# Attention stage of a four-stage kernel: the order in which SyncE writes and reads back two transposed tiles

## The chip, the cores and the metric

The kernel runs on one core of a Trainium2 chip. The metric is the device time of one execution in microseconds (us); lower is better. Engines are called PE (TensorE), DVE (VectorE), ACT (ScalarE), POOL (GpSimd) and SP (SyncE). SP computes nothing; it waits on semaphores and issues DMAs.

## The reference

The program is a chain of four residual blocks on x of shape (2, 2048, 256): a gated scan, a feed-forward block with ternary weights, a second-order linear attention, and the feed-forward block again. The change lies in the attention (16 heads of 64, here with T = 2048):

```python
def step(carry, qkv):
    S_K, C_QV, G = carry
    q_t, k_t, v_t = qkv
    k_C = jnp.einsum('bhk,bhkv->bhv', k_t, C_QV)
    G = G + k_t[..., :, None] * k_C[..., None, :]
    S_K = S_K + k_t[..., :, None] * k_t[..., None, :]
    C_QV = C_QV + q_t[..., :, None] * v_t[..., None, :]
    S_C = jnp.einsum('bhkj,bhjv->bhkv', S_K, C_QV)
    o_t = jnp.einsum('bhk,bhkv->bhv', q_t, S_C - G)
    return ((S_K, C_QV, G), o_t)
_, outs = jax.lax.scan(step, (S_K0, C_QV0, G0), (q, k, v))
```

## The kernel before, in words

The attention is computed in 32 chunks of 64 tokens (`CHUNKS`), both batch entries and all 8 pairs of heads at once. For chunk j, PE first computes scores A from the keys and queries (`scores_of`, L1187) in `first_group`, then the products with the two running states (`by_states`, L1198 and L1202), then `u_and_s` (L1213), which gives u and the change of the state S. DVE masks scores A (`mask_scores`, L1599), ACT copies u^T out of PSUM into `ut` (L1486). Between these parts PE computes the projections of keys, queries and values for coming chunks, and the output product of an earlier chunk (`out_product`, L1247 to L1249). After `u_and_s` come `o_by_scores` (L1224) and scores B (L1187 again). The change of the state Z (`change_z`, L1235) for chunk j is computed at the start of chunk j + 2.

Two operands are needed with tokens on partitions, while they are computed with features on partitions: the keys of each chunk, and u. Both are transposed in two steps. DVE transposes within blocks of 32x32 (`turn_keys(j + 1)`, L1609, and `turn_u(j)`, L1616, in that order, in each chunk j). SP then moves the blocks: it writes the turned tile of 512 KB to a scratch tensor in DRAM with one DMA (`save_k`, `save_u`, both L1063), waits until that has landed, and reads it back with four DMAs of 128 KB (`land_k`, `land_u`, both L1069). ACT at last copies the landed blocks into their places (L1497): `store_k_rows(j)` writes `krow`, which `u_and_s(j)` reads, and `store_u_rows(j - 1)` writes `urow`, which `change_z(j - 1)` reads in chunk j + 1.

Keys are written from and read back into the same tile (`k32`; the trace calls it `k`, the rows of instruction order `k_75`). The turned u lies in `turned`, which is the same memory as scores A (`sc_and_k` in the rows); so DVE's first masking of scores A in chunk j + 1 waits until the write of u of chunk j is over (`u_saved`).

All of this is written out by hand as one in-order program for each engine, with counting semaphores between them; nothing reorders it. On SP, in chunk j, the order is: write the keys of j + 1, write u of j, read back the keys of j + 1, read back u of j. Each step begins with its own wait: L1062 for the DVE transposes, L1067 for the write.

In an odd chunk j the keys of chunk j + 1 have only just been projected when DVE turns them, shortly ahead of u. In an even chunk j they come out of a projection of the chunk before, and DVE turns them several us ahead of u.

Of the kernel before, what the change touches and what calls it, by code (L numbers as in the profile page):

```python
# [25 lines left out]
CHUNKS = T // CHUNK  # L26
# [10 lines left out]
def hybrid_kernel(nc, x_d, gamma_d, wqkva_d, wq_d, wk_d, wv_d, wo_d, w1_d, b1_d, w2_d, b2_d, out_d):  # L37
# [12 lines left out]
    with outer:  # L50
# [68 lines left out]
        def rows(b, i, c=0, n=1):  # L119

            return xres[:, bass.ds((i * CH + (b * TILES + c)) * D, n * D)]
# [818 lines left out]
        def attention(before):  # L940
# [58 lines left out]
            LAST_STATE = CHUNKS - 1  # L999
# [59 lines left out]
            def sync(sp):  # L1059
                def save_turned(scratch, tile, ready, saved, count):  # L1060

                    sp.wait_ge(ready, 2 * (count + 1))  # L1062
                    sp.dma_start(scratch, tile.rearrange("p t m d -> p t (m d)")).then_inc(saved, 16)  # L1063

                def land_rows(scratch, tile, saved, landing, count):

                    sp.wait_ge(saved, 16 * (count + 1))  # L1067
                    for t in range(4):
                        sp.dma_start(tile[t * 32:(t + 1) * 32, :, :, :].rearrange("p r m d -> p r (m d)"),  # L1069
                                     scratch.rearrange("(r p) t c -> t p r c", r=4)[t]).then_inc(landing, 16)  # L1070

                def save_k(j):
                    save_turned(rows_dram["k"], k32, k_turned, k_saved, j)

                def land_k(j):
                    land_rows(rows_dram["k"], k32, k_saved, k_landed, j)

                def save_u(j):
                    if j:
                        sp.wait_ge(u_landed, 64 * j)  # L1080
                    save_turned(rows_dram["u"], turned, u_turned, u_saved, j)

                def land_u(j):
                    if j:
                        sp.wait_ge(urow_done, 2 * j)
                    land_rows(rows_dram["u"], landed, u_saved, u_landed, j)

                save_k(0)
                land_k(0)
                for j in range(CHUNKS):  # L1090
                    if j + 1 < CHUNKS:
                        save_k(j + 1)
                    if j < LAST_STATE:
                        save_u(j)
                    if j + 1 < CHUNKS:
                        land_k(j + 1)
                    if j < LAST_STATE:
                        land_u(j)
                    if j == CHUNKS - 4:
                        sp.wait_ge(q_ready, 4 * KQ_BLOCKS)  # L1100
                        sp.dma_start(w1t_again[:, :, :].rearrange("p a b -> p (a b)").bitcast(FP32), w1t_dram).then_inc(w1_loaded, 16)
                sp.wait_ge(v_ready, 2 * CHUNKS)
                sp.dma_start(wv_hi[:, :, :].rearrange("p a b -> p (a b)").bitcast(FP32), w2t_dram).then_inc(w2_loaded, 16)
                for i in range(NBLK):
                    for b in range(B):
                        for j in range(2):
                            sp.wait_ge(d_xadd[b], 2 * i + j + 1)
                            sp.dma_start(out_view[b, :, i * CH + 2 * j:i * CH + 2 * j + 2, :],
                                         rows(b, i, 2 * j, 2).rearrange("p (n d) -> p n d", d=D)).then_inc(stored, 16)
                sp.wait_ge(w1_loaded, 16)  # L1110
                sp.wait_ge(w2_loaded, 16)
                sp.wait_ge(wq_loaded, 32)
                sp.wait_ge(stored, 16 * 2 * B * NBLK)
                sp.wait_ge(k_landed, 64 * CHUNKS)
                sp.wait_ge(u_landed, 64 * LAST_STATE)
# [479 lines left out]
            def vector(dve):  # L1595
# [186 lines left out]
                for j in range(2):  # L1782
                    add_down(TASKS - 1, j)

            return Stage(sync, gpsimd, tensor, scalar, vector)


# [68 lines left out]
```

## Time and profile before

| | |
|---|---|
| median of 3 runs | 1033.69 us (1032.54 to 1034.43) |
| profiled execution, its own time | 1031.72 us |
| its span in the trace | 1030.0 us |
| granted TensorE clock | 1.00 throughout |
| PE busy | 1003.6 us, 97% |
| DVE, ACT busy | 616.6 us, 491.8 us |
| mean share of the 16 DMA engines | 28.0% for the data queue |

The span counts from the first to the last instruction in the trace; the execution's own time is 1.72 us longer. Attention takes about 240 to 900 us of the span, with a chunk every 20 to 21 us. "Issue" in the chain of work and in the waits is idle time of PE for which the trace knows no semaphore.

### The profile page before, as it was taken

To read this page: it belongs to the slowest core of one execution; us is meant where nothing else is said; L and a number is where in the kernel's file an instruction comes from. 1 tells how busy PE (TensorE), PEld (TensorE's weight loads), DVE (VectorE), ACT (ScalarE), POOL (GpSimd) and SP (SyncE) were. 2 spreads that over 40 slices of the span, in tenths; PEclk is the share of its full clock that TensorE was granted. 3 is DMA by queue.
4 is the path that set the end of the run, shared out by engine and by line. 5 is a ranking of instruction groups with operands and counts; after the bars stand their busy time and mean duration, and the time that the engine had idled before them with its cause. 6 is when DMAs were issued, how large, how long until landed. Compare 5 with 4: busy or idle time off the path is not lost.

```text
span 1030.0 us, 41963 instructions
## 1 busy us (share of the span) xinstructions
PE 1003.6 (97%) x19166; PEld 906.8 (88%) x19166; DVE 616.6 (60%) x1252; ACT 491.8 (48%) x925; POOL 111.5 (11%) x130
## 2 busy tenths in 40 slices
PE   8999999999999999999999999999999999999998
PEld 6888798999988998899889989998899988889897
DVE  7888877763445544555465554563564457767773
ACT  5676766643343433343444334333443344456663
POOL 2461331220000000000000000000000000113130
PEclk9999999999999999999999999999999999999999
DMA  9422000023324323342234233422343343200101
GB/s 316 154 57 82 1 2 1 1 83 111 119 85 121 110 85 105 105 122 89 85 120 131 86 105 105 126 85 85 105 138 93 106 125 110 80 22 21 42 31 52
DMA packets 60735, 92.75 MB, mean 90 GB/s; under 512 B 7056, under 2 KB 50448, under 8 KB 59536
## 3 DMA queue, kind: packets, MB, share of 16 engines
q1 hardware_dynamic: 60288, 90.07, 28.0%
q8 instruction: 151, 2.47, 1.0%
q14 instruction: 24, 0.20, 0.1%
q10 hardware_dynamic: 272, 0.00, 0.0%
HBM read 48.63 MB, written 41.42 MB: 87 GB/s over the span
## 4 chain that ended last, share of the span: by engine, by line
PE 94%; DVE 2%; ACT 2%; issue 2%; DMA 0%; POOL 0%; SPq 0%; ACTq 0%; DVEq 0%; POOLq 0%
PE bank L223 7%; PE bank L224 6%; PE bank L225 6%; PE bank L1187 6%; PE bank L1213 6%; PE bank L1198 5%; PE bank L1247 4%; PE bank L1235 3%; PE bank L1177 3%; PE bank L1224 3%; PE bank L805 3%; PE bank L807 3%; PE bank L1248 3%; PE bank L1249 3%; PE bank L1263 3%; PE bank L1179 3%
## 5 line engine op out<-in xcount | busy, mean ns | idle before, releaser
L1473 ACT COPY qt<-bank 128x512 f32<-128x512 f32 x64 | 37.6, 587 | 149.3 <-PE bank L225 149.3
L1609 DVE STREAM_TRANSPOSE k<-kt 128x512 f32<-128x512 f32 x64 | 43.4, 697 | 108.8 <-ACT kt L1468 59.0
L1468 ACT COPY kt<-bank 128x512 f32<-128x512 f32 x64 | 37.6, 587 | 116.5 <-PE bank L225 116.5
L1630 DVE TENSOR_TENSOR state_s<-bank,state_s 128x256 f32<-128x256 f32 x124 | 46.7, 419 | 73.5 <-ACT ut L1486 71.5
L1247 PE MATMUL bank<-wo_hi,ot_hi 128*128 128x256 f32 x256 | 74.9, 293 | 0.8 <-issue 0.8
L223 PE MATMUL bank<-ln_xhi,wq_hi 128*128 128x256 f32 x256 | 75.4, 295 | 0.0
L223 PE MATMUL bank<-ln_xhi,wk_hi 128*128 128x256 f32 x256 | 75.2, 294 | 0.0
L1198 PE MATMUL bank<-qt,state_s 64*64 64x64 f32 x2048 | 69.5, 220 | 3.2 <-issue 3.2
L1623 DVE TENSOR_TENSOR state_z<-bank,state_z 128x512 f32<-128x512 f32 x62 | 39.9, 685 | 54.4 <-PE bank L1235 54.3
L1520 ACT ACTIVATE D_hidden<-bank,b_sb 128x512 f32<-128x512 f32 x64 | 44.1, 690 | 59.3 <-PE bank L1264 59.3
L224 PE MATMUL bank<-ln_xlo,wq_hi 128*128 128x256 f32 x256 | 72.4, 283 | 0.1
L225 PE MATMUL bank<-ln_xhi,wq_lo 128*128 128x256 f32 x256 | 72.3, 282 | 0.0
L1202 PE MATMUL bank<-qt,state_z 64*64 64x64 f32 x2048 | 70.2, 221 | 1.7 <-issue 1.7
L224 PE MATMUL bank<-ln_xlo,wk_hi 128*128 128x256 f32 x256 | 71.8, 281 | 0.0
L225 PE MATMUL bank<-ln_xhi,wk_lo 128*128 128x256 f32 x256 | 71.7, 280 | 0.0
L1248 PE MATMUL bank<-wo_lo,ot_hi 128*128 128x256 f32 x256 | 71.6, 280 | 0.0
L1198 PEld LDWEIGHTS bank<-qt,state_s 64*64 64x64 f32 x2048 | 64.5, 135 | 7.9 <-issue 3.9
L1249 PE MATMUL bank<-wo_hi,ot_lo 128*128 128x256 f32 x256 | 71.3, 279 | 0.0
L898 DVE TENSOR_TENSOR B_hid_lo<-B_hidden,B_hid_hi 128x512 fp32r<-128x512 f32 x64 | 54.7, 877 | 21.3 <-ACT B_hid_hi L844 21.1
L1202 PEld LDWEIGHTS bank<-qt,state_z 64*64 64x64 f32 x2048 | 64.9, 135 | 2.4 <-issue 2.1
L805 PE MATMUL bank<-w2t,B_hid_hi 128*128 128x256 f32 x256 | 63.0, 282 | 0.7 <-DVE B_hid_lo L898 0.7
L857 ACT ACTIVATE B_hidden<-bank,b_sb 128x512 f32<-128x512 f32 x64 | 44.2, 692 | 39.1 <-PE bank L788 26.0
(161 smaller groups left out, 2919.3 us busy)
## 6 DMA issues: line engine op xcount, KB each, us to landing
k_rows_scratch<-k SPq DMA_DIRECT2D x32, 512.0 KB, 2.9
k<-k_rows_scratch SPq DMA_DIRECT2D x128, 128.0 KB, 3.5
u_rows_scratch<-sc_and_k SPq DMA_DIRECT2D x31, 512.0 KB, 3.1
landed<-u_rows_scratch SPq DMA_DIRECT2D x124, 128.0 KB, 3.3
out_dram<-xres SPq DMA_DIRECT2D x16, 256.0 KB, 2.1
xres<-in_L_attn_a_x_dram SPq DMA_DIRECT2D x7, 512.0 KB, 9.8
w_nat<-in_L_ffn_W_dram SPq DMA_DIRECT2D x2, 1024.0 KB, 9.6
raw<-in_L_attn_b_W_q_dram SPq DMA_DIRECT2D x1, 1024.0 KB, 12.1
```

Of the source, the lines that this page charges most:

```text
L223: nc.tensor.matmul(out, w_hi, x_hi, start=(k == 0), stop=False)
L224: nc.tensor.matmul(out, w_hi, x_lo, start=False, stop=False)
L225: return nc.tensor.matmul(out, w_lo, x_hi, start=False, stop=(k == last_k))
L805: nc.tensor.matmul(dst, hid_hi[:, b, f, c * P:(c + 1) * P], w2t[:, f, :], start=(f == 0), stop=False)
L898: nc.vector.tensor_tensor(hid_lo[:, b, f, :], hidden[:, f % 4, :], hid_hi[:, b, f, :].bitcast(FP32), ALU.subtract).then_inc(hlow_done, 1)
L1187: last = nc.tensor.matmul(bank[bank_of[h]][half(b), p * CHUNK:(p + 1) * CHUNK], keys(p, h, b), qt[half(h), j // 2 % 2, p, j % 2, b, :], st ...
L1198: last = nc.tensor.matmul(bank[UB[b][p // 4]][half(h), u_cols(p, 0)], state_s[half(h), b, p, :], qt[half(h), j // 2 % 2, p, j % 2, b, :], ...
L1202: last = nc.tensor.matmul(bank[OB[b]][half(1 - h), cols], state_z[half(h), b, p, :], qt[half(h), (j - 1) // 2 % 2, p, (j - 1) % 2, b, :], ...
L1213: last = nc.tensor.matmul(bank[UB[b][p // 4]][half(h), u_cols(p, 0, n)], krow[half(b), p, half(h)], sc_and_k[half(b), 0:n, p, h, :], start ...
L1247: nc.tensor.matmul(dst, ot_hi[:, p, :], w[0], start=(p == 0), stop=False)
L1248: nc.tensor.matmul(dst, ot_hi[:, p, :], w[1], start=False, stop=False)
L1249: last = nc.tensor.matmul(dst, ot_lo[:, p, :], w[0], start=False, stop=(p == PAIRS - 1))
```

## The change

On SP, in each chunk, the four reads of the turned keys are moved ahead of the write of u. No instruction is added or removed on any engine, and no other engine's program changes.

```diff
                 for j in range(CHUNKS):
                     if j + 1 < CHUNKS:
                         save_k(j + 1)
+                        land_k(j + 1)
                     if j < LAST_STATE:
                         save_u(j)
-                    if j + 1 < CHUNKS:
-                        land_k(j + 1)
-                    if j < LAST_STATE:
                         land_u(j)
```

The next rows are SP's instructions in chunks 0 and 1 of the loop, as a difference between the two kernels (`k_75` is the keys' tile, `landed` the one into which u is read back).

```order
 L1063 DMA k_rows_scratch<-k_75 128x1024 [waits C_kturned]
+L1069 DMA k_75<-k_rows_scratch 32x4x256 [waits C_ksaved]
+L1069 DMA k_75<-k_rows_scratch 32x4x256 x3
 L1063 DMA u_rows_scratch<-sc_and_k 128x1024 [waits C_uturned]
-L1069 DMA k_75<-k_rows_scratch 32x4x256 [waits C_ksaved]
-L1069 DMA k_75<-k_rows_scratch 32x4x256 x3
 L1069 DMA landed<-u_rows_scratch 32x4x256 [waits C_usaved]
 L1069 DMA landed<-u_rows_scratch 32x4x256 x3
```

The wait for the keys' write (`C_ksaved`) and the four reads behind it now stand ahead of the wait for the turned u (`C_uturned`) and of u's write.

The same place in every later chunk, first before and then of the changed kernel; u's write waits there for its read of the chunk before as well (`C_uland`), and its reads for the copies out of `landed` (`C_urow`).

```order
L1063 DMA k_rows_scratch<-k_75 128x1024 [waits C_kturned]
L1063 DMA u_rows_scratch<-sc_and_k 128x1024 [waits C_uturned,C_uland]
L1069 DMA k_75<-k_rows_scratch 32x4x256 [waits C_ksaved]
L1069 DMA k_75<-k_rows_scratch 32x4x256 x3
L1069 DMA landed<-u_rows_scratch 32x4x256 [waits C_usaved,C_urow]
L1069 DMA landed<-u_rows_scratch 32x4x256 x3
```

```order
L1063 DMA k_rows_scratch<-k_75 128x1024 [waits C_kturned]
L1069 DMA k_75<-k_rows_scratch 32x4x256 [waits C_ksaved]
L1069 DMA k_75<-k_rows_scratch 32x4x256 x3
L1063 DMA u_rows_scratch<-sc_and_k 128x1024 [waits C_uturned,C_uland]
L1069 DMA landed<-u_rows_scratch 32x4x256 [waits C_usaved,C_urow]
L1069 DMA landed<-u_rows_scratch 32x4x256 x3
```

Here too only the four reads of the keys have moved, past one write.

## Rows read from the trace of the kernel before

**Rows 1.** The page: busy time, and the chain that ended last by engine

```profile
PE 1003.6 (97%) x19166; PEld 906.8 (88%) x19166; DVE 616.6 (60%) x1252; ACT 491.8 (48%) x925; POOL 111.5 (11%) x130
...
PE 94%; DVE 2%; ACT 2%; issue 2%; DMA 0%; POOL 0%; SPq 0%; ACTq 0%; DVEq 0%; POOLq 0%
```

**Rows 2.** PE's waits, 220 to 880 us: total us, times, longest

```profile
PE bank L1187 <- issue: 5.0, 3, 1.9
PE bank L1198 <- issue: 3.2, 3, 1.5
PE bank L1202 <- issue: 1.7, 3, 0.9
```

**Rows 3.** Chain of work in order of time: start us, length us, what

```profile
300.10 0.92 issue
...
421.29 1.42 issue
509.37 0.82 issue
...
711.16 1.90 issue
800.21 0.45 issue
```

**Rows 4.** DMA issues of the page: KB each, median us to landing

```profile
k_rows_scratch<-k SPq DMA_DIRECT2D x32, 512.0 KB, 2.9
k<-k_rows_scratch SPq DMA_DIRECT2D x128, 128.0 KB, 3.5
u_rows_scratch<-sc_and_k SPq DMA_DIRECT2D x31, 512.0 KB, 3.1
```

**Rows 5.** Timeline of SP, 505 to 545 us (chunks 13 and 14)

```profile
514.95 0.34 SPq L1063 DMA_DIRECT2D k_rows_scratch<-k  x1
517.95 0.34 SPq L1063 DMA_DIRECT2D u_rows_scratch<-sc_and_k  x1
518.33 2.28 SPq L1069 DMA_DIRECT2D k<-k_rows_scratch  x4
521.18 2.80 SPq L1069 DMA_DIRECT2D landed<-u_rows_scratch  x4
531.51 0.34 SPq L1063 DMA_DIRECT2D k_rows_scratch<-k  x1
538.95 0.34 SPq L1063 DMA_DIRECT2D u_rows_scratch<-sc_and_k  x1
539.33 2.38 SPq L1069 DMA_DIRECT2D k<-k_rows_scratch  x4
```

**Rows 6.** Timeline of DVE, the same stretch

```profile
526.65 1.28 DVE L1599 TENSOR_TENSOR sc_and_k<-bank,causal 128x512 f32<-128x512 f32 x2
...
537.57 1.29 DVE L1616 STREAM_TRANSPOSE sc_and_k<-ut 128x512 f32<-128x512 f32 x2
```

**Rows 7.** ACT, 220 to 880 us: its wait, and two copies of the timeline

```profile
ACT sc_and_k L1497 <- DMA k<-k_rows_scratch: 10.2, 10, 3.7
...
525.01 1.14 ACT L1497 COPY sc_and_k<-k 128x512 f32<-128x512 f32 x2
...
537.03 1.16 ACT L1497 COPY urow<-landed 128x512 f32<-128x512 f32 x2
```

**Rows 8.** Timelines of SP and DVE, 838 to 905 us (chunk 30)

```profile
869.66 0.34 SPq L1063 DMA_DIRECT2D k_rows_scratch<-k  x1
872.37 0.34 SPq L1063 DMA_DIRECT2D u_rows_scratch<-sc_and_k  x1
...
878.90 1.28 DVE L1599 TENSOR_TENSOR sc_and_k<-bank,causal 128x512 f32<-128x512 f32 x2
```

**Rows 9.** Busy by stretch, 290 to 840 us, and instruction packets in it

```profile
290.00:840.00 550.00, 540.73 (x14115) 497.26 (x14119) 287.37 (x575) 216.25 (x434) 8.50 (x14) 1.00 0.35 106
...
q8 instruction: 112, 1.84, 1.4%
```

**Rows 10.** Timeline, chunk 12: u's write on SP, PE behind its gap

```profile
496.79 0.34 SPq L1063 DMA_DIRECT2D u_rows_scratch<-sc_and_k  x1
...
510.19 0.21 PE L1198 MATMUL bank<-qt,state_s 64*64 64x64 f32 x1 [0.82 <-issue]
```

## The prediction

> **What bounds the kernel now.** I read the page first. PE is busy for 97% of the span and makes up 94% of the chain that ended last; DMA and SP's queue have 0% of that chain [rows 1]. So a change in SP's order can save only what PE loses, and cost only what PE does not lose yet.
>
> Next I read PE's own waits in the attention, 220 to 880 us. Three lines with nine waits hold 5.0 + 3.2 + 1.7 = 9.9 us, all "issue" [rows 2]. No semaphore is behind them. The chain of work in order of time says where they are; five of the pieces are at 300.10, 421.29, 509.37, 711.16 and 800.21 us [rows 3].
>
> What are they? From 290 to 840 us PE ran 14115 matmuls and 14119 weight loads, and the DMA view counts 112 packets of the kind "instruction", 1.84 MB, in the same stretch [rows 9]. That is 28234 / 112 = 252 PE instructions and 16 KB per packet: PE's program is fed through the DMA engines, a packet every 4.9 us on average. The gap before L1198 at 510.19 us stands in the middle of a run of identical matmuls, so no operand can be missing there [rows 10]. I take the gaps to be PE at the end of its fed instructions: a packet came late while the data queue was full, and the short 64x64 matmuls of `by_states` and of the scores then ate the rest. This reading is an inference, and the rest of my forecast hangs on it.
>
> The third view is SP's timeline of two chunks. In odd chunk 13 the keys' write goes out at 514.95, u's write at 517.95, the keys' reads at 518.33 and take 2.28 us to issue, u's reads at 521.18 us. In even chunk 14 the keys' write goes out at 531.51, u's at 538.95, and the keys' reads only at 539.33 us, though their data had been in DRAM for some 4.5 us [rows 5].
>
> **The change part by part.** No instruction is added, so all costs are shifts in time.
>
> *Keys in even chunks.* A 512 KB keys' write lands 2.9 us after its issue and a read 3.5 us after its own [rows 4]. The reads would be issued at 531.51 + 3.0 = 534.5 instead of 539.33, 4.8 us earlier, and be landed by 534.5 + 2.3 + 3.5 = 540.3. The only reader is ACT's copy into `krow` in the next chunk; it waited for these DMAs ten times, 10.2 us in total, at most 3.7 [rows 7]. ACT's waits are not on the path: PE waits on no ACT copy of L1497 in rows 2. Worth: 0 us, at most 10.2 us off ACT's idle time.
>
> *u in even chunks.* The reads are issued over by 536.8, and u is turned at 537.57 + 1.29 = 538.86 [rows 6], so u's write still goes at 538.95. Worth 0 us.
>
> *u in odd chunks.* The wait for the keys' write ends at 514.95 + 3.0 = 517.95; four reads at 2.28 us push u's write to 520.2 or 520.3, 2.3 us later than now. Behind it on SP stand u's reads and the next chunk's keys' write; the latter waits for DVE until 531.51 and has room. Who waits for u's write: DVE's mask of scores A in chunk 14, which starts at 526.65 [rows 6]. The write takes 3.1 us [rows 4], so it is over at 523.4, 3.2 us in time. Who waits for u's reads: ACT's copy at 537.03 [rows 7]; issued from 523.4 over 2.8 us and landed by 529.7, they have 7 us left. Worth 0 us; if that cover were gone, it would cost DVE, and a masking that is late has still a projection on PE between itself and `u_and_s`.
>
> *The tightest place is chunk 30,* where projections run out: keys' write at 869.66, hence u's write at 869.66 + 3.0 + 2.3 = 875.0 instead of 872.37, over at 878.1; the mask starts at 878.90 [rows 8]. 0.8 us is left. If the write took 1 us more, the price would be 0.2 us, once.
>
> *Keys in odd chunks.* Reads go 0.4 us earlier and no longer behind u's 512 KB. ACT's copy of them at 525.01 [rows 7] needs nothing sooner. 0 us.
>
> *The feed of PE's instructions.* Here the order matters. Today u's write, the keys' reads and u's reads form one unbroken burst in every chunk. In even chunks the change takes the keys' reads out of it and puts them where the queue is empty; u's write has then nothing behind it for 3.1 us. In odd chunks the burst is 2.3 us longer, since SP issues keys' reads before u's write where it had both in flight together. The trace of before has no row for an instruction packet against a u write alone. The bounds for even chunks: nothing (the packet waits for the write as before), or the packet comes earlier by as much as the issue of the keys' reads takes, 2.3 us [rows 5], which would close all five gaps of rows 3. By SP's timeline these five follow even chunks; they sum to 0.92 + 1.42 + 0.82 + 1.90 + 0.45 = 5.5 us. I take 0.6 us for each, an estimate: the packet no longer waits for the part of the keys' reads that is in flight with u's write, a quarter of the 2.3 us; 4 x 0.6 + 0.45 = 2.8 us saved. For odd chunks, the other about 4 gaps in the 9.9 us can grow by as much as the burst grows, 2.3 us each, or shrink since their burst is thinner; I take +0.25 each, +1.0 us. Sum: -2.8 + 1.0 = -1.8 us.
>
> Against the profiled execution: 1031.72 - 1.8 = 1029.9 us. That execution is 1.97 us below the median of 1033.69, so runs like those shown should have a median of 1031.9 us.
>
> A rule of the Trainium skill speaks against this term. "Runtime: NRT & Kernel Launch", section "Instruction fetch mechanics", says that instructions are fetched ahead in 16 KiB blocks over a DMA queue of the sequencer's own, and that crossing a block boundary is mostly hidden. The trace agrees on the block (1.84 MB in 112 packets [rows 9]); of "hidden" it leaves 9.9 us in nine waits uncovered [rows 2], if my reading of them holds. By the rule the term would be 0 and the sum 1031.72 us.
>
> **The rivals.**
>
> *A, the forecast:* gaps shrink by 1 to 3.5 us in sum, median 1031.9, own range 1030.2 to 1032.9. For it: the gaps exist, and in half the chunks the DMA work is spread out. Against: 1.8 us is of the size of the spread of the runs shown (1.9 us).
>
> *B, nothing but the order on SP:* the packet's wait depends on the writes alone, or gaps are only re-dealt. 1033.7, within 0.8 us. For it: both 512 KB writes stay, and every user of both tiles has room as worked out above. "DMA: Bandwidth & Descriptors" in the Trainium skill, section "Queues, rings and completion order", says that each DMA engine takes turns between the queues with work, packet by packet; by that an instruction packet waits for one data packet, however many stand behind, and the result is B. No row here separates the turns of single engines.
>
> *C, slower:* in odd chunks u's reads run from 523.4 to about 529.7 instead of from 521.18 to 527.5, right up to the start of `by_states` of the next chunk, the fastest consumer of instructions. There are 15 of them from chunk 1 to 29. If half (7) then lose 0.6 us each, that is +4.2; with A's even half at no gain, the median is 1037.9; with it, 1035.1. It decides from the point where more than 3 of the odd chunks lose a gap of the size of rows 3's mean, 1.1 us. Against it: by then the data packets are reads of 128 KB each, and in the trace of before the gaps are not more frequent after the longer burst.
>
> *D, more is freed:* a u write without reads behind lets the packet pass at once, all five even gaps close: -5.5, and with +1.0 from odd ones 1029.2.
>
> **How the numbers follow.** A has 0.50, B 0.28, C 0.12, D 0.10. From no change a measurement of this kernel can tell about 0.2%, 2.1 us. A ends beyond it in some 0.4 of its cases: 0.20, with all of D 0.30, and I add 0.06 of B and A for a draw of the runs: faster 0.36. Slower: C and 0.01 of B: 0.13. Within 0.2%: 0.51. The range of 1029.5 to 1035.2 holds A, B, the mild end of C and the upper half of D.
>
> **What would show it.** Right: in even chunks the keys' reads stand at 3.0 us behind their write and 4 us ahead of u's write; in odd chunks u's write moves from 3.0 to 5.3 us behind the keys'; ACT's wait of 10.2 us for the keys' reads shrinks to under 2; no wait of DVE for SP's writes appears; PE's "issue" waits in the attention fall from 9.9 to about 8 us. Wrong: "issue" waits that stay or grow, a DVE wait before L1599 of scores A, or a u write in odd chunks that comes more than 3 us later.

## The result, and the profile after

The changed kernel is faster by half a percent: 1028.73 us median of 8 runs (1026.75 to 1031.44) against 1034.19 us of 8 runs before (1032.54 to 1036.41), ratio 0.9951 with a 95% interval of 0.9936 to 0.9967. I had forecast 1031.9 us, range 1029.5 to 1035.2, and put 0.36 on faster. The direction was that of my central estimate, the size was not: the time lies 0.8 us below my range, and the saving is 5 us where I had worked out 1.8.

The page of the changed kernel (lines below the edit have moved up by two, so L1187 is now L1185, and so on), its chain by engine, the data queue's share and the DMA issues:

```profile
PE 1005.3 (98%) x19166; PEld 909.2 (88%) x19166; DVE 617.2 (60%) x1252; ACT 491.0 (48%) x925; POOL 111.4 (11%) x130
...
q1 hardware_dynamic: 60288, 90.07, 26.6%
...
PE 95%; ACT 2%; issue 1%; DVE 1%; POOL 0%; POOLq 0%; ACTq 0%; DVEq 0%
...
k_rows_scratch<-k SPq DMA_DIRECT2D x32, 512.0 KB, 2.7
k<-k_rows_scratch SPq DMA_DIRECT2D x128, 128.0 KB, 2.9
u_rows_scratch<-sc_and_k SPq DMA_DIRECT2D x31, 512.0 KB, 3.4
```

The bytes are the same, but the 16 DMA engines are busy for 26.6% of the span instead of 28.0% (26.5% and 28.3% in the second traces). The keys' reads land in 2.9 us instead of 3.5, while u's write takes 3.4 instead of 3.1 [rows 4]. Next, SP's timeline in chunks 13 and 14:

```profile
513.02 0.34 SPq L1063 DMA_DIRECT2D k_rows_scratch<-k  x1
515.73 1.82 SPq L1069 DMA_DIRECT2D k<-k_rows_scratch  x4
517.64 0.38 SPq L1063 DMA_DIRECT2D u_rows_scratch<-sc_and_k  x1
521.28 1.73 SPq L1069 DMA_DIRECT2D landed<-u_rows_scratch  x4
529.57 0.34 SPq L1063 DMA_DIRECT2D k_rows_scratch<-k  x1
532.99 1.73 SPq L1069 DMA_DIRECT2D k<-k_rows_scratch  x4
537.02 0.34 SPq L1063 DMA_DIRECT2D u_rows_scratch<-sc_and_k  x1
540.09 2.15 SPq L1069 DMA_DIRECT2D landed<-u_rows_scratch  x4
```

The order stands as forecast, the distances nearly so: in the odd chunk u's write goes 4.6 us behind the keys' write, where I had forecast 5.3, instead of 3.0 [rows 5]. From the keys' write to the last read the burst of that chunk grows by 1.0 us (513.02 to 523.01, before 514.95 to 523.98), and not by the 2.3 us that I had forecast. In the even chunk the keys' reads have moved into the quiet stretch ahead of u's write. PE's, ACT's and DVE's waits in the attention, 220 to 880 us (total, times, longest):

```profile
PE bank L1185 <- issue: 5.7, 4, 2.0
PE bank L1196 <- issue: 1.7, 2, 1.1
...
PE bank L1200 <- issue: 0.9, 1, 0.9
...
ACT sc_and_k L1495 <- DMA k<-k_rows_scratch: 4.2, 4, 2.2
...
DVE sc_and_k L1597 <- DMA u_rows_scratch<-sc_and_k: 0.4, 1, 0.4
```

PE's waits without a semaphore are 8.3 us, against 9.9 for the same three lines before [rows 2] (10.7 with 0.8 at L1247). ACT's wait for the keys' reads is 4.2 us, where I had forecast under 2. DVE waits 0.4 us for u's write, once. But the two profiled executions are a poor pair: 1031.72 us lies under every timed run before, 1030.74 us lies above the median after. In addition a stretch of the changed kernel's trace ran at half clock. Busy times and, third column from the right, the granted clock:

```profile
709.00:711.00 2.00, 0.00 (x1) 0.00 (x0) 1.00 (x2) 0.00 (x0) 0.00 (x0) 1.00 0.00 0
711.00:714.50 3.50, 3.50 (x16) 3.34 (x16) 0.69 (x1) 0.37 (x1) 0.00 (x0) 0.51 0.02 5
714.50:720.00 5.50, 5.50 (x158) 5.30 (x157) 0.71 (x1) 2.42 (x5) 0.00 (x0) 1.00 0.02 4
```

PE sat idle for 2.0 us in one "issue" gap and then had 0.51 of full speed (1.2 instead of 2.4 GHz) for 3.4 us. Half of that, 1.7 us, is lost on top of the gap, an estimate from the two levels.

### The profile page after: what moved, and what is told of

It is laid out like the page before. It is cut to its first block, busy times and chain, and to the rows that moved or that the text cites. A ratio compares the mean times of both kernels' runs of the same rounds, so it can differ in the third digit from the quotient of the medians.

```text
span 1029.0 us, 41963 instructions
## 1 busy us (share of the span) xinstructions
PE 1005.3 (98%) x19166; PEld 909.2 (88%) x19166; DVE 617.2 (60%) x1252; ACT 491.0 (48%) x925; POOL 111.4 (11%) x130
## 3 DMA queue, kind: packets, MB, share of 16 engines
q1 hardware_dynamic: 60288, 90.07, 26.6%
## 4 chain that ended last, share of the span: by engine, by line
PE 95%; ACT 2%; issue 1%; DVE 1%; POOL 0%; POOLq 0%; ACTq 0%; DVEq 0%
PE bank L223 7%; PE bank L224 6%; PE bank L1185 6%; PE bank L225 6%; PE bank L1211 6%; PE bank L1196 5%; PE bank L1245 4%; PE bank L1233 3%; PE bank L1175 3%; PE bank L1222 3%; PE bank L805 3%; PE bank L807 3%; PE bank L1246 3%; PE bank L1247 3%; PE bank L1261 3%; PE bank L1177 3%
## 5 line engine op out<-in xcount | busy, mean ns | idle before, releaser
L1247 PE MATMUL bank<-wo_hi,ot_lo 128*128 128x256 f32 x256 | 71.3, 279 | 0.0
L1200 PE MATMUL bank<-qt,state_z 64*64 64x64 f32 x2048 | 70.0, 221 | 1.0 <-issue 0.9
L1200 PEld LDWEIGHTS bank<-qt,state_z 64*64 64x64 f32 x2048 | 64.7, 135 | 1.5 <-issue 1.3
L807 PE MATMUL bank<-w2t,B_hid_lo 128*128 128x256 f32 x256 | 62.8, 281 | 0.0
## 6 DMA issues: line engine op xcount, KB each, us to landing
xres<-in_L_attn_a_x_dram SPq DMA_DIRECT2D x7, 512.0 KB, 10.5
```

Source lines behind the costliest of these rows:

```text
L807: last = nc.tensor.matmul(dst, hid_lo[:, b, f, c * P:(c + 1) * P], w2t[:, f, :], start=False, stop=(f == FC - 1))
L1200: last = nc.tensor.matmul(bank[OB[b]][half(1 - h), cols], state_z[half(h), b, p, :], qt[half(h), (j - 1) // 2 % 2, p, (j - 1) % 2, b, :], ...
L1247: last = nc.tensor.matmul(dst, ot_lo[:, p, :], w[0], start=False, stop=(p == PAIRS - 1))
```

## The experiments

Below, "issue" is the sum of PE's waits without a semaphore between 220 and 880 us in the one profiled execution of a kernel. It varies from one execution to the next (10.7 and 15.1 us in the two traces of the kernel before), so it shows large differences only. Ratios are against the kernel before, interleaved on the same chip, with their 95% interval; they can differ from the quotient of the two medians by up to 0.0013. In all 19 traces of this study the span, less "issue", less PE's waits of 2.0 us for DVE in one of them, less 1.7 us for each 3.4 us piece at half clock in the attention, comes to 1018.0 to 1020.8 us, while the spans themselves go from 1023.0 to 1036.3. So most of what differs between these kernels, and between executions of one of them, is in those terms.

**The two kernels again.** The files unchanged.

> The changed kernel once more, for a second trace and time. Both theories: ratio 0.993 to 0.997. Feed theory (PE runs out of fed instructions when the data queue is full): PE's issue waits in the attention again 2 us or more below those of the kernel before of the same chip. Clock theory (the difference lies in the granted clock): issue waits equal, and the mean clock of the faster kernel is higher.

> The kernel before against itself: ratio 1.000 within 0.2%. Feed theory: its trace shows issue waits of 10 us or more in the attention, where its first trace, which was faster than all its timed runs, showed 10.7 us with the small group at L1247.

Measured: the changed kernel 0.9951 (0.9934 to 0.9968), 1029.36 us; the kernel before against itself 1.0011 (0.9989 to 1.0033), 1035.44 us. PE's waits in the second trace of the kernel before:

```profile
PE bank L1187 <- issue: 7.0, 5, 1.9
PE bank L1198 <- issue: 3.8, 3, 1.5
PE bank L1202 <- issue: 2.8, 3, 1.2
PE bank L1247 <- issue: 1.1, 1, 1.1
...
PE bank L1235 <- issue: 0.4, 1, 0.4
```

That is 15.1 us, at a span of 1034.6; the second trace of the changed kernel has 7.6 us at 1029.5. Neither trace of before is typical: the first ran 2.5 us below the median of 8 runs, the second, at 1036.34 us, 0.9 above the median of its 12. The first understated the term, by up to a third. The clock theory fails as the main cause: the changed kernel's profiled execution has the lower mean clock (0.997 against 1.000) and is still faster, and over all timed executions of this round the mean clocks are 0.9978 and 0.9973. I estimate from these that the clock makes 0.5 us of the 5.

The same traces settle what the gaps are, better than my one look at a gap inside a run of identical matmuls did. I count PE's recorded matmuls and weight loads, with its sequencer's instructions, from the start of the span. All 181 "issue" gaps in the attention, in all 19 traces, stand where this number is 193 above a multiple of 256, and the whole trace has 38735 of these instructions to 151 packets of the queue `q8 instruction`, 256.5 each. Each time PE starts again 2.1 to 3.1 us after the start of a packet of this queue, and each time PE stands 449 instructions past 256 times the number of packets that had started before that one. So PE does stop at the end of its supplied instructions, and the gap ends when the next packet is in. The packets start later where there is more data: from the moment at which PE is 160 instructions past a multiple of 256 to the start of the next packet it takes 1.72 and 1.77 us on average in the two traces before, 1.55 and 1.54 in the changed kernel's, and, in kernels described below, 1.29 without the data and 1.88 with one more write.

The count also names each gap. These are the five gaps on which I had put my saving, and two of the others (us, from first and second trace):

| PE instructions done | at about, us | before | changed |
|---|---|---|---|
| 6081 | 300 | 0.92, 1.25 | none, none |
| 12225 | 420 | 1.42, 1.69 | 1.69, 1.69 |
| 16833 | 509 | 0.82, 1.10 | none, none |
| 27329 | 711 | 1.90, 1.90 | 2.00, 1.73 |
| 31937 | 800 | 0.45, 1.00 | none, 0.72 |
| 6849 | 316 | 1.67, 1.93 | 1.10, 0.57 |
| 33985 | 840 | 1.52, 1.52 | 0.61, 1.49 |

The first five sum to 5.5 and 6.9 us before, and to 3.7 and 4.1 after; the rest of "issue" to 5.2 and 8.2 before, and to 4.6 and 3.5 after.

**One half of the change at a time.** `early` was `j % 2 == 0` in one kernel, `j % 2 == 1` in the other.

```diff
-                    if j + 1 < CHUNKS:
-                        save_k(j + 1)
+                    early = j % 2 == 0
+                    if j + 1 < CHUNKS:
+                        save_k(j + 1)
+                        if early:
+                            land_k(j + 1)
                     if j < LAST_STATE:
                         save_u(j)
-                    if j + 1 < CHUNKS:
+                    if j + 1 < CHUNKS and not early:
                         land_k(j + 1)
```

> The keys' reads go ahead of u's write in even chunks alone. Feed theory: the gain comes from taking the reads out of the burst behind u's write, which is here done without pushing u's write back in odd chunks: ratio 0.993 to 0.997, at least as fast as the full change. Rival (u's write with nothing in flight beside it in odd chunks matters): half or less of the gain, 0.998.

> The keys' reads go ahead of u's write in odd chunks alone. Feed theory: u's write goes 2 us later and the burst is longer but thinner, nothing gained: 0.999 to 1.001, at worst 1.002. Rival (the odd chunks carry it): 0.996.

Measured: even 0.9967 (0.9949 to 0.9985), "issue" 9.9 us; odd 0.9960 (0.9944 to 0.9977), "issue" 10.9 us. Both halves gain, 3.4 and 4.1 us by these ratios; together they give 5.1, less than the sum, but by no more than the intervals allow. My expectation for odd chunks was wrong, as the prediction's term for them had been.

**No data in the transfers.** Every DMA of both tiles moves 16 elements of each row it touched, or of the first of them. All waits stay; POOL also clears `landed` once, and SP and ACT wait for that at the start. The attention's result is left out.

```diff
-                    sp.dma_start(scratch, tile.rearrange("p t m d -> p t (m d)")).then_inc(saved, 16)
+                    sp.dma_start(scratch[:, 0:1, 0:16], tile.rearrange("p t m d -> p t (m d)")[:, 0:1, 0:16]).then_inc(saved, 16)
```

> The order of before, but the writes and reads of both turned tiles move 16 elements of a row in place of 512 KB, with every wait kept; the turned rows are then not in token order, so the attention's output is left out as a result. Feed theory: without the data in the DMA engines PE's issue waits in the attention vanish but for the one of about 1.5 us beside the load of the next weights; before's traces had 10.7 and 15, so 9 to 13 us less: ratio 0.987 to 0.991. Rival (the gaps are a property of PE's program, whatever the data): issue waits of 10 us or more stay, ratio 0.999 to 1.001.

Measured: 0.9895 (0.9878 to 0.9912), 1024.85 us. PE's waits:

```profile
PE bank L1190 <- issue: 2.8, 3, 1.4
...
PE bank L1201 <- issue: 0.8, 2, 0.4
PE bank L1205 <- issue: 0.5, 2, 0.3
```

4.1 us are left. The longest, 1.4, is at 315.8 us, behind 6849 PE instructions, where each of the 19 traces has a gap. So both theories hold a part: some gaps stay without the data of these transfers, and with the data their sum is about three times as large (2.6 and 3.7 times in the two traces before). I take this saving, about 11 us, for the most that an order on SP can bring.

**More data.** The changed order and one more 512 KB write per chunk, for which nobody waits.

```diff
                         save_u(j)
                         land_u(j)
+                        sp.dma_start(extra_dram, wo_hi[:, 0:1024].bitcast(FP32)).then_inc(extra_done, 16)
```

> The changed kernel with one more 512 KB write in each of 31 chunks, of a constant tile into a scratch tensor, behind u's reads; no engine waits for it but SP at the very end. Feed theory: a longer burst brings back late packets, 3 us or more of issue waits on top of the 8 of the changed kernel: ratio 0.998 to 1.003 to the kernel before, against 0.995 of the change. Rival (the gain comes from rows landing sooner): the extra write delays no row that is used, ratio stays 0.995.

Measured: 1.0002 (0.9983 to 1.0020), "issue" 13.7 us at L1189, L1204, L1200 and L226. The extra write takes back the whole gain, though the keys' rows are in time as before (ACT waits 4.4 us for them, 4.2 in the changed kernel). So data in the DMA engines cost PE time here though nobody waited for it. The order of the keys' reads and u's write is that of the change here, and there is no gain: the order alone is not enough.

**The keys' reads last,** behind u's reads.

```diff
                     if j < LAST_STATE:
                         save_u(j)
-                    if j + 1 < CHUNKS:
-                        land_k(j + 1)
-                    if j < LAST_STATE:
                         land_u(j)
+                    if j + 1 < CHUNKS:
+                        land_k(j + 1)
```

> On SP the keys' reads go behind u's reads: keys' write, u's write, u's reads, keys' reads. Feed theory with u's write as the place where packets are held up: nothing stands behind u's write, so it gains as the change does, ratio 0.994 to 0.998. Rival one (the keys must land sooner): the keys land 3 us later than before, so the kernel is not faster, 1.000 to 1.005. Rival two (the length of the unbroken burst counts): unbroken as before, 0.999 to 1.001.

Measured: 0.9996 (0.9980 to 1.0013), "issue" 14.3 us. That is what rival two had expected, and within rival one's range. Nothing is in flight behind u's write now until it has landed, and that brings nothing: one write and eight reads still follow each other without a break. Rival one, that the keys have to land sooner, finds no support in the waits: ACT waits 70.3 us for the keys' reads here, against 10.2 in the kernel before, PE has no wait that this explains, and the time is unchanged.

**One transfer at a time.** The changed order, and `sp.wait_ge(k_landed, 64 * (j + 2))` ahead of `save_u(j)`.

> The changed order, and u's write also waits on SP until the keys' reads have landed, so that at most one transfer and its like are in flight. Feed theory: packets pass more easily still, issue waits at or below the 8 us of the changed kernel; but u's write goes 3 us later in odd chunks, over at the time at which DVE masks scores A, so DVE gets waits of 0 to 1 us for it, which a projection hides: ratio 0.992 to 0.997. Rival (DVE's mask is on the path): 1 us in each of 15 odd chunks, ratio 1.005 and more.

Measured: 1.0020 (0.9996 to 1.0043), "issue" 10.9 us. DVE and PE now wait for something new:

```profile
DVE sc_and_k L1598 <- DMA u_rows_scratch<-sc_and_k: 7.1, 6, 3.1
...
PE bank L1197 <- DVE xres L1642: 2.0, 2, 1.5
```

The cover of u's write in odd chunks, 3.2 us by my count, ends here: DVE stands for 7.1 us, 0.2 to 0.6 us in four places, 2.1 in one and 3.1 in another, and hands 2.0 of them to PE. Although u's write never shares the DMA engines with the keys' reads, the kernel is no faster than the one before; "issue" is about 3 us above the changed kernel's, a difference that two executions of one kernel can show as well. Where the changed kernel's gain goes is only in part shown: 2.0 us in PE's waits for DVE, the rest in "issue" and in one piece at half clock.

**Which transfer it is.** In the order of before, only the keys' reads shrunk; only u's write and reads; only u's reads. The last two clear `landed` first, as above. Parts of the attention's result are left out in each.

> The order of before, but the keys' reads move 16 elements of a row in place of 512 KB; the keys' rows are not in token order, so the attention's result is left out. It prices the whole of what the change can move out of the way. Feed theory: removing these reads is worth at least what moving them is worth, 0.993 to 0.996, issue waits 5 us or more below before's. If moving them did more than take their data out of the bursts (rival: the moment of u's write counts), this kernel is nearer to 1.000 than the change's 0.995.

> The order of before, but u's write and reads move 16 elements of a row in place of 512 KB; the change of state Z then uses wrong rows, so that part of the result is left out. Feed theory: two of the three transfers of the burst are gone, issue waits fall to the 4 us that remained without any of them, ratio 0.989 to 0.992. Rival (the keys' transfers alone hold packets up as much): 0.996.

> The order of before, but u's four reads move 16 elements of a row (the change of Z then uses wrong rows: that part of the result is left out); u's write stays whole. Shrinking write and reads gave 0.9897. If u's reads, which run up to the states' matmuls of the next chunk, hold the packets up: 0.990 to 0.993. If u's write does: 0.997 to 0.999.

Measured: keys' reads shrunk 0.9977 (0.9955 to 0.9998), "issue" 10.0; u's transfers shrunk 0.9897 (0.9870 to 0.9924), "issue" 4.4, the ceiling again; u's reads shrunk 0.9949 (0.9930 to 0.9967), "issue" 7.3. So u's transfers are the ones that hurt, the reads with about half of it and by difference the write with the other half, which no kernel shrunk alone. The keys' transfers alone cost nothing that shows (0.9897 against 0.9895 with theirs shrunk too). The share of the first was too small for my theory: moving the keys' reads (0.9951) brought no less than shrinking them in place, and rather more, though the intervals overlap.

**A later write of u.** Three kernels separate the reads that leave the burst from the write that goes later. The first puts five writes of 4 KB ahead of u's write in odd chunks, the second a wait (shown below), the third is the changed order with the keys' reads shrunk; it leaves parts of the attention's result out.

```diff
                         save_k(j + 1)
+                    if j % 2 and 1 < j < LAST_STATE:
+                        sp.wait_ge(x_added, j - 1)
                     if j < LAST_STATE:
                         save_u(j)
```

> The order of before; in odd chunks SP waits for the keys' write and then issues five writes of 4 KB into a scratch tensor ahead of u's write, so that u's write goes some 2 us later as in the changed kernel, while the keys' reads stay behind it. If in odd chunks it is the distance between the two 512 KB writes that lets packets through: 0.996 to 0.998. If it is the keys' reads leaving the place behind u's write: 0.999 to 1.002.

> The order of before, but in odd chunks from 3 to 29 u's write waits on SP until DVE has added the output of chunk j-2 (L1643), some 2 us later than now, with no DMA added; the keys' reads stay behind it. If in odd chunks the two 512 KB writes back to back are what holds instruction packets up: 0.996 to 0.998, as with the keys' reads ahead in odd chunks alone (0.996). If it is the place of the keys' reads: 0.999 to 1.002.

> The changed order with the keys' reads moving 16 elements of a row (the attention's result is left out). The same data as the kernel with these reads shrunk in the order of before (0.9977), but u's write in odd chunks goes about 2 us later. If the later write carries the gain: 0.993 to 0.995, at least as fast as the change. If the keys' data being out of the burst carries it: again 0.997 to 0.998, and then the change's 0.995 lies within what such a ratio is uncertain by.

Measured: 1.0031 (1.0008 to 1.0053), 1.0010 (0.9991 to 1.0028) and 0.9954 (0.9936 to 0.9971), "issue" 12.3, 12.4 and 10.8 us. The first is confounded, since its small writes are 640 more packets of 32 bytes in an odd chunk. SP's timeline in chunk 13 of the second:

```profile
515.30 0.34 SPq L1063 DMA_DIRECT2D k_rows_scratch<-k  x1
520.40 0.34 SPq L1063 DMA_DIRECT2D u_rows_scratch<-sc_and_k  x1
520.78 2.28 SPq L1069 DMA_DIRECT2D k<-k_rows_scratch  x4
525.15 1.75 SPq L1069 DMA_DIRECT2D landed<-u_rows_scratch  x4
```

Here u's write goes 5.1 us behind the keys' write instead of 3.0, with the keys' reads still behind it, and there is no gain. A later u write by itself does not pay. The third kernel has the gain of the change without the keys' data. Against the 0.9977 of the same shrunk reads in the old order this suggests that the later write pays once the reads are out of its way; it does not show it, because the two intervals overlap.

**Later still.** The changed order, and in even chunks u's write waits until DVE is through L1635, the subtraction that it runs in the chunk; then the same with the keys' reads left behind u's write; then in the changed order for all chunks from 1 to 29.

```diff
                         land_k(j + 1)
+                    if j % 2 == 0 and 0 < j < LAST_STATE - 1:
+                        sp.wait_ge(o_low, 2 * j)
                     if j < LAST_STATE:
                         save_u(j)
                         land_u(j)
```

> The changed order, and in even chunks u's write also waits until DVE has subtracted the high part of the chunk's output (L1635), 3.5 us later. It tests whether the gain is one of place in the chunk. Feed theory: u's reads then run while PE is at the states' matmuls, its fastest eater of instructions, and packets come late there: 0.998 or slower, and DVE waits for u's write up to 1 us in even chunks. If only overlap among transfers counts: 0.995 as the change.

> The order of before, but in even chunks u's write waits for DVE's subtraction (L1635), 3.5 us later, and the keys' reads stay behind it. If the moment of u's burst in even chunks is what counts: 0.996 to 0.998, the 0.3% by which that wait beat the changed order. If the keys' reads must be out of the burst for it to work: 0.999 to 1.001.

> The changed order, with u's write later in odd chunks too (up to chunk 28), until the same subtraction, some 3.7 us behind the keys' reads' issue instead of at once. If later is better wherever packets pass first: 0.988 to 0.991. If odd chunks have no room (u's write is then over about when DVE masks scores A, and its reads run into the states' matmuls): 0.992 to 0.995, DVE waits for u's write.

Measured: 0.9919 (0.9902 to 0.9936), 1025.27 us; 1.0014 (0.9997 to 1.0030); 0.9927 (0.9905 to 0.9949), 1025.36 us. The first and the third, which can't be told apart, are the fastest kernels here that compute all of the reference, 8 us below the kernel before by these ratios. The first one's SP timeline in chunk 14 and PE's waits:

```profile
529.57 0.34 SPq L1063 DMA_DIRECT2D k_rows_scratch<-k  x1
533.03 1.73 SPq L1069 DMA_DIRECT2D k<-k_rows_scratch  x4
540.57 0.34 SPq L1063 DMA_DIRECT2D u_rows_scratch<-sc_and_k  x1
543.26 1.73 SPq L1069 DMA_DIRECT2D landed<-u_rows_scratch  x4
...
PE bank L1187 <- issue: 3.1, 3, 1.1
PE bank L1202 <- issue: 1.6, 2, 1.2
PE bank L1198 <- issue: 1.6, 2, 1.1
...
DVE sc_and_k L1599 <- DMA u_rows_scratch<-sc_and_k: 0.7, 1, 0.7
```

"Issue" is 6.3 us, and no piece of the attention runs at half clock. The two long gaps that the change had left, behind 12225 and 27329 PE instructions, are 0.96 and 0.98 us here instead of 1.7 to 2.0. I had expected the reverse, with u's reads under the states' matmuls. With the keys' reads behind u's write the same wait brings nothing (13.1 us of "issue"), as in the odd chunks above. Adding odd chunks changes nothing that can be told (4.9 us of "issue", ratios within each other's intervals), though the burst of an odd chunk, from the keys' write to the last read, then lasts 11.6 us (512.59 to 524.14 in chunk 13).

## Why the prediction was right in its mechanism and wrong in one term

- *PE's "issue" gaps are the only thing that SP's order can change.* Right for the change itself. Reads of the keys that go out 5 us later, with 70.3 us of waits on ACT instead of 10.2, left the time as it was. Across 19 traces the rest of the span, taken as above, stayed within 2.8 us while "issue" went from 4.1 to 15.1. Two things lie outside: the half clock behind some gaps, and DVE's waits in the serial kernel.
- *The gaps are late instruction packets.* Right. I had argued it from one gap; the count shows it for all 181, each at the same place of a block of 256 instructions and each ended 2.1 to 3.1 us after the start of a packet. In the changed kernel's trace the packet for the 2.0 us gap starts at 708.30 us and PE starts again at 711.00. Of the 151 packets of a trace only 10 and 13 left a gap in the attention of the kernel before. The experiments show that the gaps grow and shrink with the data in the DMA engines. No run supplied PE's instructions in another way.
- *The shifts priced at 0.* Right, each, as far as PE shows it. ACT's wait for the keys fell to 4.2 us and not to under 2, and DVE waited 0.4 us in one place; neither reached PE. The serial kernel shows where the cover behind u's write in odd chunks ends.
- *The feed term, -2.8 us for even and +1.0 us for odd chunks.* The second part is the step that failed. Even chunks alone measured -3.4 us, near its size, though not as I had it: I took 0.6 us off each of four gaps and the fifth whole. In the two traces of the full change two of the five were gone, the two longest stayed as they were, and one was gone in one trace only (table above). So the size of that part came out by luck. For the odd chunks I reasoned that a burst 2.3 us longer can let the other gaps grow, or that they shrink since it is thinner, and took +0.25 us for each of four. Measured is -4.1 us for the odd half alone (0.9960), and in the traces of the full change the gaps other than those five went from 5.2 and 8.2 us to 4.6 and 3.5. The sign was wrong, and the premise too: the burst grew by 1.0 us, not by 2.3.
- *What the order does in odd chunks* stays open. Every kernel that moved all data and in which the keys' reads stood directly before or behind u's reads in all chunks, three of them with a shifted write, stayed at 1.000 to 1.003. But two kernels that had them ahead of u's write did not gain either, the one with an extra write and the serial one. Nor does the length of the burst in chunk 13 put the kernels in order: 9.0 us before, 10.0 after the change, 10.5 to 11.8 in four kernels without a gain, but 11.6 in the one with u's write late in all chunks, at 0.9927.
- *The base of 9.9 us.* I took it from an execution that was faster than all others then shown. The second trace had 15.1. Taking the two pairs of traces together, "issue" fell by 2.4 and 7.5 us, 5.0 on average, which is the saving; the forecast of "about 8 us" after the change was met (8.3 and 7.6), but from a base that was too low, with a saving too small to match.
- *Not in the sum at all:* the half clock behind some long gaps, 1.7 us a piece. By the mean clocks I estimate that it makes 0.5 us of the saving of 5 here, and about 2 us of the saving of 8 in the kernel with u's write late in even chunks (mean clock 0.9993 over its timed executions, 0.9972 of the kernel before beside it).
- *Rival B and the page behind it.* By "DMA: Bandwidth & Descriptors" in the Trainium skill, section "Queues, rings and completion order", a DMA engine takes turns between queues packet by packet, so that the data behind a packet would not count. The runs speak against that consequence: the order alone, with the same bytes, made 5 us, u's reads without their data made 5 us too (0.9949), and one more write took as much back. They do not look at the turns themselves, so the page's rule may hold and another delay stand behind it.
- *Case D* was the nearest, -5.5 and a total of 1029.2 us, at 0.10. Its reason, that a u write without reads behind lets all five even gaps close, does not hold: two of the five stayed, and the kernel with the keys' reads last has such a write and gains nothing. Its number is near by luck.

What stays open besides: why a later u write in even chunks helps once the keys' reads are away. It fits that the packet due when PE enters its fast matmuls then passes ahead of the write, but no run separated that from u's reads moving away from those matmuls.

## What to carry to other kernels

When an engine is busy for 97% of the span, look at its waits that no semaphore explains before calling an off-path transfer free: here DMA traffic that PE never waited for cost 11 us. Count the engine's instructions up to such gaps: if all counts share one remainder by the size of an instruction packet, the engine is waiting for its program. In a program of many short matmuls try moving unrelated reads ahead of a large write, and holding the write back by a wait. Measure each such order: of those tried here, as many did nothing as helped. Size such a term from several executions, since one trace can be off by a third.

## What the runs showed of the hardware that I had not expected

- Removing nearly all the data of the two tiles' transfers, for which PE never waited, saved 10.9 us (0.9895), and 4.1 us of "issue" waits stayed.
- All 181 "issue" gaps of PE in 19 traces stand 193 instructions past a multiple of 256, and end 2.1 to 3.1 us after the start of an instruction packet.
- The same bytes kept the DMA engines busy for 26.6% instead of 28.0% of the span after four reads moved past one write.
- An idle gap of 2.0 us on PE was followed at once by 3.4 us at 0.51 of full clock. The first trace of the kernel before has a gap of 1.90 us at 711.16 [rows 3] and the full clock behind it. In the attention of the 19 traces 14 such pieces of 3.4 us stand within 1.5 us of the end of a gap of 1.7 to 2.5 us; 24 other gaps of that length have none.
